# A 16-image hybrid network on one core: the first attention's instructions in another order, and layer-norm statistics written without a copy

## The chip, the core and the metric

The kernel runs on one core of one Trainium2 chip. The time is the device time of one execution in microseconds (us). TensorE (PE) does the matrix products, VectorE (DVE), ScalarE (ACT) and GpSimd (POOL) the elementwise work, SyncE (SP) issues DMAs. Each engine works through its own list of instructions in order; only semaphores order the lists against one another.

## The reference, cut to what matters

Sixteen images of 16x16 tokens with 96 channels pass six blocks: windowed attention with MLP, a convolution mixer with MLP, full attention, a binary FFN, causal attention, and four experts. The change touches the first block, and the statistics of most of the others. The first block is, for each image:

```
h = layernorm(x) * w + b                      # over 96 channels
windows of 8x8 tokens: 4 per image, 64 tokens each
qkv = h @ qkv_w + qkv_b                       # 12 heads of 8 channels
attn = softmax(q @ k^T / sqrt(8) + bias)      # 64 x 64 per head, bias by relative position
x = x + (attn @ v) @ proj_w + proj_b
```

Every later block begins with a layer norm of the new x, so each block, on adding its result to x, also takes mean and variance of it.

## The kernel before

**Layout.** x stays in SBUF as X, 32 tiles of 128 tokens; an image is two tiles. MV holds mean and variance of each tile. `statistics` (line 181) takes them after a residual has been added: per tile a bn_stats of X into stats, then per tile a bn_aggr into the small tile aggr, then, after a wait, one copy of aggr into MV, which raises the semaphore mv. `image_stats` (line 397) does the same for the input images of the first block, on semaphores of its own. GpSimd's `normalise` (line 138) waits for mv.

**The first attention** (`window_attention`, line 412) runs in half images. A half image u (0 to 31) is two windows, 128 rows; image n = u // 2. All engines run an outer loop over slots u, written out in full; in slot u each works on several images at different depths. By name:
- GpSimd `norm(n)`: the layer norm of image n into Y, then the projection's bias added to X (five instructions). The subtraction (line 463) takes the row maxima off the scores of u.
- TensorE `tokens_t(n)`: two transposes of Y into bank 0. `queries_keys(n)`: two projections into bank 1. `values(n)`: eight matmuls into bank 1. `scores(u)`: 12 matmuls into banks 3 to 5. `probs_t(u, b)`: three transposes of the probabilities (b = 0, 1: bank 6 or 2). `attend(u)`: 24 matmuls into bank 7. `outputs_t(n)`: two transposes into bank 0. `project(n)`: into bank 0.
- ScalarE: `tokens`, `queries`, `values`, `pt_out`, `out_t` copy these results out of the banks, and `exps(u)` is the exponential.
- VectorE: `keys_by_head(n)` spreads the keys over four masked copies. `biased_scores(u)` adds the position bias and then takes the maxima (lines 662 and 665). `heads_out(u)` divides by the sums. `residual(n)` adds the projection to X.

**Waits that matter here.** `tokens_t(n)` writes bank 0, which the projection of image n-4 still fills until its residual is read:

```
pe.wait_ge(s["y"], n + 1)
after(pe, s["hT"], n)
after(pe, s["x"], n - 4)
```

`scores(u)` waits until the add of u-1 has read banks 3 to 5, and the add of u waits for scores u. `values(n)` waits for queries n, which wait for the keys of n. `outputs_t(n)` waits for both heads of n. `project(n)` waits for out_t of n.

**Per image on VectorE before**, slot 2n and then 2n+1: image_stats n+4, residual n-3, add and maxima 2n, statistics n-3, heads 2n-3; add and maxima 2n+1, heads 2n-2, keys n+2.

**Per image on TensorE before**: scores 2n, both probs_t of 2n-2, attend 2n-3, tokens_t n+2, values n+1; scores 2n+1, probs_t of 2n-1 (first half), outputs_t n-2, probs_t (second half), queries_keys n+2, attend 2n-2, project n-2.

**Other users of statistics**: the two MLP stages (four tiles a step, in a hardware loop), the conv mixer (line 990, between two of the nine taps of the convolution on VectorE, ahead of `norm2`, whose chain runs over GpSimd's reciprocal root, `norm2b`, TensorE's `back` and ScalarE to the output matmuls and so to the next residual), the full attention (line 1304), the binary FFN (line 1478) and the causal attention (lines 1892 and 1905).

Of the kernel before, what the change touches and what calls it, by code (L numbers as in the profile page):

```python
# [22 lines left out]
ALU = mybir.AluOpType  # L23
# [114 lines left out]
def tiles_of(t, first, count):  # L138

    return t[:, bass.ds(first, count), :]  # L140
# [39 lines left out]

def statistics(dve, k, s, n, count):

    alone(dve, k)
    dve.wait_ge(s["x"], n + 1)
    after(dve, s["mv"], n)
    for t in range(count):
        last = dve.bn_stats(k.stats[:, t, :], k.X[:, bass.ds(n * count + t, 1), :])
    last.then_inc(s["bn"], 1)
    alone(dve, k)
    dve.wait_ge(s["bn"], n + 1)  # L190
    for t in range(count):
        last = dve.bn_aggr(k.aggr[:, t, :], k.stats[:, t, :])
    last.then_inc(s["ag"], 1)
    dve.wait_ge(s["ag"], n + 1)
    dve.tensor_copy(tiles_of(k.MV, n * count, count), k.aggr[:, 0:count, :]).then_inc(s["mv"], 1)
# [201 lines left out]
def image_stats(dve, k, s, i):  # L397

    dve.wait_ge(s[f"x{i // 4}"], 16 * 2 * WS)
    for t in range(2):  # L400
        last = dve.bn_stats(k.stats[:, t, :], k.X[:, 2 * i + t, None, :])
    last.then_inc(s["bn"], 1)
    dve.wait_ge(s["bn"], i + 1)
    for t in range(2):
        last = dve.bn_aggr(k.aggr[:, t, :], k.stats[:, t, :])
    last.then_inc(s["ag"], 1)
    dve.wait_ge(s["ag"], i + 1)
    dve.tensor_copy(tiles_of(k.MV, 2 * i, 2), k.aggr[:, 0:2, :]).then_inc(s["mv"], 1)
    dve.wait_ge(s["mv"], i + 1)


def window_attention(k, bank, begin):
# [3 lines left out]
    with ExitStack() as ctx:  # L416
# [19 lines left out]
        with nc.Block() as block:  # L436
# [8 lines left out]
            def _(pool):  # L445
# [13 lines left out]
                norm(2)  # L459
                for u in range(HALVES):  # L460
                    pool.wait_ge(s["mx"], u + 1)
                    x = S[u % 4]
                    pool.tensor_tensor(x[:], x[:], mx[u % 4][:].broadcast_to([P, H0, WTOK]), ALU.subtract).then_inc(s["sub"], 1)  # L463
                    if u % 2 == 0 and u // 2 + 3 < IMAGES:
                        norm(u // 2 + 3)
                pool.wait_ge(s["late"], 16 * len(k.late))
# [3 lines left out]
            def _(pe):  # L470
# [80 lines left out]
                for u in range(FIRST, LAST + 1):  # L551
# [3 lines left out]
                    if 0 <= u - 2 < HALVES:  # L555
                        probs_t(u - 2, 0)
                    if odd and 0 <= n - 2 < IMAGES:
                        outputs_t(n - 2)
                    if 0 <= u - 2 < HALVES:
                        probs_t(u - 2, 1)  # L560
                    if odd and n + 2 < IMAGES:
# [11 lines left out]
            def _(act):  # L573
# [38 lines left out]
                for u in range(FIRST, LAST + 1):  # L612
                    n, odd = u // 2, u % 2 == 1
                    if 0 <= u - 1 < HALVES:
                        exps(u - 1)
                    if not odd and 0 <= n + 1 < IMAGES:
                        queries(n + 1)
                    if 0 <= u - 2 < HALVES:
                        pt_out(u - 2, 0)
                    if odd and 0 <= n - 2 < IMAGES:  # L620
                        out_t(n - 2)
                    if 0 <= u - 2 < HALVES:
                        pt_out(u - 2, 1)
                    if not odd and n + 2 < IMAGES:
                        tokens(n + 2)
                    if not odd and 0 <= n + 1 < IMAGES:
                        values(n + 1)

            @block.vector
            def _(dve):  # L630
# [17 lines left out]
                def keys_by_head(n):  # L648
# [5 lines left out]
                                             op0=ALU.add, op1=ALU.mult).then_inc(s["kx"], 1)  # L654

                def biased_scores(u):
                    x = S[u % 4]
                    dve.wait_ge(s["sc"], u + 1)
                    if u == 0:
# [3 lines left out]
                                      k.bias0[:].rearrange("p (g j) k -> p g (j k)", g=3), ALU.add).then_inc(s["add"], 1)  # L663
                    dve.wait_ge(s["add"], u + 1)
                    dve.tensor_reduce(mx[u % 4][:, :, 0], x[:], AX.X, ALU.max).then_inc(s["mx"], 1)  # L665

# [12 lines left out]
                next(run)  # L679
                for u in range(FIRST, LAST + 2):  # L680
                    n, odd = u // 2, u % 2 == 1
                    if not odd and 3 <= n + 4 < IMAGES:
                        image_stats(dve, k, k.sem["set"], n + 4)
                    if not odd and 0 <= n - 3 < IMAGES:
                        residual(n - 3)
                    if 0 <= u < HALVES:
                        biased_scores(u)
                    if not odd and 0 <= n - 3 < IMAGES:
                        statistics(dve, k, s, n - 3, 2)
                    if 0 <= u - 3 < HALVES:  # L690
                        heads_out(u - 3)
                    if odd and n + 2 < IMAGES:
                        keys_by_head(n + 2)


def mlp(k, bank, prefix, w):
# [4 lines left out]
    with ExitStack() as ctx:  # L701
        G = [k.sb(f"{prefix}_G{i}", [P, KH, 512], F32, ctx) for i in range(2)]
        with nc.Block() as block:
# [44 lines left out]
            def _(dve):  # L748
                def residual(n):
                    dve.wait_ge(s["down"], n + 1)  # L750
                    dve.wait_ge(s["xb"], n + 1)
                    add_and_stats(dve, k, s, n, 4, bank[7][:, 0:4 * C].rearrange("p (t c) -> p t c", t=4))

# [1470 lines left out]
```

## Time and profile before

| what | value |
|---|---|
| time, median of 3 runs | 1306.49 us (1303.2 to 1314.98) |
| the profiled execution | 1309.46 us |
| its span, first to last instruction | 1307.7 us |
| mean granted TensorE clock | 0.942 of 2.4 GHz |
| TensorE busy | 1154.8 us (88%) |
| VectorE busy | 740.0 us (57%) |
| ScalarE busy | 515.9 us (39%) |
| GpSimd busy | 387.1 us (30%) |

The profiled execution is one run, 1.76 us longer than its span. The first attention lies from about 17 to 188 us in it, the first MLP to 247, the conv mixer to 407, the second MLP to 465, the full attention to 826, the binary FFN to 918, the causal attention and the experts to the end. A busy share over the span mixes stages with different limits. In the timeline a row is a start, a length, an engine and a line of the kernel; in brackets how long the engine sat idle before it, and which instruction's end ended that.

### The profile page before, as it was taken

What the parts mean: (1) busy time and instruction counts of PE and PEld (TensorE: products, weight loads), DVE (VectorE), ACT (ScalarE), POOL (GpSimd) and SP (SyncE); (2) the same over time, 40 slices, a digit from 0 to 9 for tenths busy, and PEclk for the clock granted to TensorE, in tenths of its full rate; (3) what the DMA queues carried; (4) which work ended last, traced back from release to release, by engine and by line L of the source; (5) the groups of instructions that cost most, each with busy time, mean ns of one, the idle gap of its engine ahead of it and who ended that gap; (6) DMA issues with size and microseconds to landing.
All of it is one profiled execution on the core that took longest, in us unless ns stands there. A gap on an engine that the chain in (4) does not pass through costs nothing. (4 is left out here: it accounts for less than half of the span.)

```text
span 1307.7 us, 23695 instructions
## 1 busy us (share of the span) xinstructions
PE 1154.8 (88%) x8859; PEld 790.6 (60%) x8859; DVE 740.0 (57%) x2112; ACT 515.9 (39%) x839; POOL 387.1 (30%) x584
## 2 busy tenths in 40 slices
PE   4888879789887979999999997788888978999998
PEld 2565656566665656766666674466455544577776
DVE  3788844477772436666666666276455565333322
ACT  1555533343431333333343332345343422455543
POOL 3645445443425421010101210424100000353522
PEclk8999969899997989999999998699799999999999
DMA  4500000000000000000000000000000000000000
GB/s 88 100 11 2 2 2 0 1 1 1 2 1 1 0 1 1 1 1 1 1 1 1 1 2 1 1 1 1 1 2 1 2 2 1 2 13 7 9 11 13
DMA packets 28924, 9.39 MB, mean 7 GB/s; under 512 B 26961, under 2 KB 28816, under 8 KB 28816
## 3 DMA queue, kind: packets, MB, share of 16 engines
q1 hardware_dynamic: 25760, 7.02, 2.6%
q8 instruction: 69, 1.13, 0.3%
q10 hardware_dynamic: 3056, 0.92, 0.3%
q14 instruction: 39, 0.32, 0.1%
HBM read 6.36 MB, written 1.57 MB: 6 GB/s over the span
## 5 line engine op out<-in xcount | busy, mean ns | idle before, releaser
L156 POOL TENSOR_TENSOR ln_v<-MV,eps 128x2 f32<-128x2 f32 (+3 forms) x81 | 16.2, 201 | 427.2 <-PE bank L1132 247.3
L1194 ACT ACTIVATE fa_e<-bank 128x1024 f32<-128x1024 f32 x64 | 65.5, 1024 | 161.1 <-PE bank L1102 161.1
L1997 PEld LDWEIGHTS bank<-e_w,ex_G 128*128 128x128 f32 x768 | 90.6, 192 | 14.4 <-issue 14.1
L2112 DVE SCALAR_TENSOR_TENSOR X<-bank,ex_L,X 128x96 f32<-128x96 f32 x128 | 31.8, 311 | 114.0 <-PE bank L1997 108.1
L1246 DVE TENSOR_REDUCE fa_z<-bank 128x4 f32<-128x1024 f32 x64 | 78.3, 1223 | 26.3 <-PE bank L1084 24.7
L1989 PE MATMUL bank<-hT,e_w 96*128 96x512 f32 x192 | 90.6, 609 | 0.0
L1997 PE MATMUL bank<-e_w,ex_G 128*128 128x96 f32 x768 | 90.0, 274 | 0.0
L2040 ACT ACTIVATE ex_G<-bank,e_b 128x512 f32<-128x512 f32 x96 | 64.3, 686 | 61.7 <-PE bank L1989 58.9
L1844 DVE TENSOR_REDUCE ca_z<-bank 128x2 f32<-128x256 f32 x96 | 48.9, 552 | 49.3 <-PE bank L1571 49.2
L1102 PE MATMUL bank<-fa_a,fa_b 64*128 64x256 f32 x512 | 74.1, 409 | 1.1 <-DVE fa_a L1253 1.1
L1115 PE MATMUL bank<-fa_e,fa_v 128*64 128x256 f32 x512 | 72.0, 404 | 1.1 <-ACT fa_e L1194 1.1
L159 POOL TENSOR_TENSOR ln_r<-ln_v,minus_half 128x2 f32<-128x2 f32 (+3 forms) x81 | 71.7, 885 | 0.0
L1762 ACT ACTIVATE ca_e<-bank 128x768 f32<-128x768 f32 x48 | 38.9, 810 | 78.9 <-PE bank L1571 78.9
L463 POOL TENSOR_TENSOR wa_s<-wa_s,wa_mx 128x768 f32<-128x768 f32 x32 | 47.1, 1471 | 73.8 <-DVE wa_mx L665 73.8
L1010 DVE SCALAR_TENSOR_TENSOR cm_acc<-cm_g,k_conv,cm_acc 128x256 f32<-128x256 f32 x128 | 66.1, 516 | 3.0
L1084 PE MATMUL bank<-fa_b,fa_a 64*128 64x256 f32 x512 | 66.0, 376 | 0.1
L1102 PEld LDWEIGHTS bank<-fa_a,fa_b 64*128 64x128 f32 x512 | 45.0, 190 | 29.4 <-issue 24.6
L1943 POOL TENSOR_TENSOR ex_tmp<-e_b,ex_L 128x384 f32<-128x384 f32 x8 | 6.7, 833 | 185.7 <-DVE ex_L L2100 185.7
L1557 PE MATMUL bank<-ca_b,ca_a 16*128 16x256 f32 (+1 forms) x384 | 47.4, 366 | 16.1 <-DVE ca_a L1853 15.7
L163 POOL TENSOR_TENSOR Y<-Y,ln_r 128x192 f32<-128x192 f32 (+3 forms) x81 | 56.1, 693 | 10.9
L1253 DVE TENSOR_TENSOR fa_a<-fa_a,bank 128x256 f32<-128x256 f32 x64 | 26.9, 421 | 56.3 <-PE bank L1092 56.3
L178 DVE TENSOR_TENSOR X<-X,bank 128x192 f32<-128x192 f32 (+2 forms) x56 | 23.6, 427 | 61.8 <-PE bank L719 43.0
(252 smaller groups left out, 2641.7 us busy)
## 6 DMA issues: line engine op xcount, KB each, us to landing
out_tokens<-X SPq DMA_DIRECT2D x8, 192.0 KB, 2.1
X<-in_x SPq DMA_DIRECT2D x56, 24.0 KB
e_w<-in_L_ffn_w SPq DMA_DIRECT2D x2, 576.0 KB
bias0r<-in_L_conv_rpb_table ACTq DMA_DIRECT2D x16, 24.0 KB
m0w<-in_L_conv_mlp_w SPq DMA_DIRECT2D x2, 144.0 KB
m1w<-in_L_conv_w SPq DMA_DIRECT2D x2, 144.0 KB
f_w<-in_L_ffn_W SPq DMA_DIRECT2D x2, 142.5 KB
mixer<-in_mixer SPq DMA_DIRECT2D x1, 256.0 KB
```

The source lines that it names most:

```text
L159: pool.tensor_tensor(r, v, k.minus_half[:, 0:count, :], ALU.pow).then_inc(s["rstd"], 1)
L163: pool.tensor_tensor(y, y, r.broadcast_to([P, count, C]), ALU.mult).then_inc(s["y"], 1)
L1010: dve.scalar_tensor_tensor(out=o, in0=src, scalar=kk, in1=o, op0=ALU.mult, op1=ALU.add).then_inc(s["conv"], 1)
L1084: last = pe.matmul(bank[b + i][:, c * TOK:(c + 1) * TOK], A[n % 2][rows, p, c * P:(c + 1) * P], B[n % 2][rows, p, :], start=True, stop=True)
L1102: last = pe.matmul(bank[b + i][:, c * TOK:(c + 1) * TOK], B[n % 2][rows, p, c * P:(c + 1) * P], A[n % 2][rows, p, :], start=True, stop=True)
L1115: last = pe.matmul(bank[4 + v % 2][64 * i:64 * i + 64, 0:TOK], V[n % 2][:, c, 2 * p + i, :], E[v % 2][:, i, c, :], start=(c == 0), stop=(c ...
L1194: act.activation(E[v % 2][:], k.banks[:, b:b + 2, :].rearrange("p i (c q) -> p i c q", c=2), ACT.Exp).then_inc(s["exp"], 1)
L1246: dve.tensor_reduce(Z[v % 2][:].rearrange("p c (i d) -> p i c d", i=2)[:, :, :, D2], k.banks[:, b:b + 2, :].rearrange("p i (c q) -> p i c ...
L1844: last = dve.tensor_reduce(dst, k.banks[:, 2 * p:2 * p + 2, c * P:(2 * c + 1) * P], AX.X, ALU.max, negate=True)
L1989: pe.matmul(bank[v % NB][:], k.ew1[:, e, j * P:(j + 1) * P], k.hT[slot][:], start=True, stop=True).then_inc(s["up"], 1)
L1997: last = pe.matmul(bank[4 + e % 2][:, t * C:(t + 1) * C], G[e % 2][:, j, t * P:(t + 1) * P], k.ew2[:, e, j, :], start=(j == 0), stop=(j == ...
L2040: act.activation(G[e % 2][:, j, :], bank[(KH * e + j) % NB][:], ACT.Gelu, bias=k.eb1[:, e, j:j + 1]).then_inc(s["gelu"], 1)
```

## The change

In the first attention, the lists are rearranged:
- VectorE, slot 2n: heads 2n-4, add 2n, keys n+1, maxima 2n, residual n-3; slot 2n+1: heads 2n-3, add and maxima 2n+1, statistics n-3, image_stats n+4. `maxima` becomes a function of its own.
- TensorE: outputs_t follows both halves of probs_t.
- ScalarE, slot 2n: pt_out (first half), exps 2n-1, pt_out (second half), queries n+1, tokens n+2; slot 2n+1: values n+1, pt_out, exps 2n, pt_out, out_t n-2.
- GpSimd: norm is written ahead of the subtraction of odd slots instead of behind that of even ones.

In `statistics` and `image_stats` bn_aggr writes straight into MV and raises mv; aggr, its wait and the copy fall away, except where `unrolled=False` is passed, which the MLP stages do. `image_stats` uses tiles 6 and 7 of stats.

```diff
@@ -178,7 +178,7 @@
     (dve.tensor_copy(x, new) if replace else dve.tensor_tensor(x, x, new, ALU.add)).then_inc(s["x"], 1)
 
 
-def statistics(dve, k, s, n, count):
+def statistics(dve, k, s, n, count, unrolled=True):
 
     alone(dve, k)
     dve.wait_ge(s["x"], n + 1)
@@ -188,6 +188,11 @@
     last.then_inc(s["bn"], 1)
     alone(dve, k)
     dve.wait_ge(s["bn"], n + 1)
+    if unrolled:
+        for t in range(count):
+            last = dve.bn_aggr(k.MV[:, n * count + t, :], k.stats[:, t, :])
+        last.then_inc(s["mv"], 1)
+        return
     for t in range(count):
         last = dve.bn_aggr(k.aggr[:, t, :], k.stats[:, t, :])
     last.then_inc(s["ag"], 1)
@@ -397,16 +402,14 @@
 def image_stats(dve, k, s, i):
 
     dve.wait_ge(s[f"x{i // 4}"], 16 * 2 * WS)
+    after(dve, s["mv"], i)
     for t in range(2):
-        last = dve.bn_stats(k.stats[:, t, :], k.X[:, 2 * i + t, None, :])
+        last = dve.bn_stats(k.stats[:, 6 + t, :], k.X[:, 2 * i + t, None, :])
     last.then_inc(s["bn"], 1)
     dve.wait_ge(s["bn"], i + 1)
     for t in range(2):
-        last = dve.bn_aggr(k.aggr[:, t, :], k.stats[:, t, :])
-    last.then_inc(s["ag"], 1)
-    dve.wait_ge(s["ag"], i + 1)
-    dve.tensor_copy(tiles_of(k.MV, 2 * i, 2), k.aggr[:, 0:2, :]).then_inc(s["mv"], 1)
-    dve.wait_ge(s["mv"], i + 1)
+        last = dve.bn_aggr(k.MV[:, 2 * i + t, :], k.stats[:, 6 + t, :])
+    last.then_inc(s["mv"], 1)
 
 
 def window_attention(k, bank, begin):
@@ -458,11 +461,11 @@
                 next(run)
                 norm(2)
                 for u in range(HALVES):
+                    if u % 2 == 1 and u // 2 + 3 < IMAGES:
+                        norm(u // 2 + 3)
                     pool.wait_ge(s["mx"], u + 1)
                     x = S[u % 4]
                     pool.tensor_tensor(x[:], x[:], mx[u % 4][:].broadcast_to([P, H0, WTOK]), ALU.subtract).then_inc(s["sub"], 1)
-                    if u % 2 == 0 and u // 2 + 3 < IMAGES:
-                        norm(u // 2 + 3)
                 pool.wait_ge(s["late"], 16 * len(k.late))
                 next_first_step(pool, k, s, IMAGES)
 
@@ -554,10 +557,10 @@
                         scores(u)
                     if 0 <= u - 2 < HALVES:
                         probs_t(u - 2, 0)
+                    if 0 <= u - 2 < HALVES:
+                        probs_t(u - 2, 1)
                     if odd and 0 <= n - 2 < IMAGES:
                         outputs_t(n - 2)
-                    if 0 <= u - 2 < HALVES:
-                        probs_t(u - 2, 1)
                     if odd and n + 2 < IMAGES:
                         queries_keys(n + 2)
                     if 0 <= u - 3 < HALVES:
@@ -611,20 +614,20 @@
                 act.wait_ge(s["pad"], 1)
                 for u in range(FIRST, LAST + 1):
                     n, odd = u // 2, u % 2 == 1
+                    if odd and 0 <= n + 1 < IMAGES:
+                        values(n + 1)
+                    if 0 <= u - 2 < HALVES:
+                        pt_out(u - 2, 0)
                     if 0 <= u - 1 < HALVES:
                         exps(u - 1)
+                    if 0 <= u - 2 < HALVES:
+                        pt_out(u - 2, 1)
+                    if odd and 0 <= n - 2 < IMAGES:
+                        out_t(n - 2)
                     if not odd and 0 <= n + 1 < IMAGES:
                         queries(n + 1)
-                    if 0 <= u - 2 < HALVES:
-                        pt_out(u - 2, 0)
-                    if odd and 0 <= n - 2 < IMAGES:
-                        out_t(n - 2)
-                    if 0 <= u - 2 < HALVES:
-                        pt_out(u - 2, 1)
                     if not odd and n + 2 < IMAGES:
                         tokens(n + 2)
-                    if not odd and 0 <= n + 1 < IMAGES:
-                        values(n + 1)
 
             @block.vector
             def _(dve):
@@ -653,6 +656,10 @@
                                              scalar=k.bk0[:], in1=k.headmask[:, :, None].broadcast_to([C, G4, TOK]),
                                              op0=ALU.add, op1=ALU.mult).then_inc(s["kx"], 1)
 
+                def maxima(u):
+                    dve.wait_ge(s["add"], u + 1)
+                    dve.tensor_reduce(mx[u % 4][:, :, 0], S[u % 4][:], AX.X, ALU.max).then_inc(s["mx"], 1)
+
                 def biased_scores(u):
                     x = S[u % 4]
                     dve.wait_ge(s["sc"], u + 1)
@@ -661,8 +668,6 @@
                     after(dve, s["pt"], 2 * u - 6)
                     dve.tensor_tensor(x[:].rearrange("p (g j) k -> p g (j k)", g=3), k.banks[:, 3:6, 0:G4 * WTOK],
                                       k.bias0[:].rearrange("p (g j) k -> p g (j k)", g=3), ALU.add).then_inc(s["add"], 1)
-                    dve.wait_ge(s["add"], u + 1)
-                    dve.tensor_reduce(mx[u % 4][:, :, 0], x[:], AX.X, ALU.max).then_inc(s["mx"], 1)
 
                 run = begin.vector(dve)
                 next(run)
@@ -677,20 +682,22 @@
                     last = dve.memset(t[C:P], 0.0)
                 last.then_inc(s["pad"], 1)
                 next(run)
-                for u in range(FIRST, LAST + 2):
+                for u in range(FIRST, LAST + 1):
                     n, odd = u // 2, u % 2 == 1
-                    if not odd and 3 <= n + 4 < IMAGES:
-                        image_stats(dve, k, k.sem["set"], n + 4)
+                    if 0 <= u - 4 < HALVES:
+                        heads_out(u - 4)
+                    if 0 <= u < HALVES:
+                        biased_scores(u)
+                    if not odd and 0 <= n + 1 < IMAGES:
+                        keys_by_head(n + 1)
+                    if 0 <= u < HALVES:
+                        maxima(u)
                     if not odd and 0 <= n - 3 < IMAGES:
                         residual(n - 3)
-                    if 0 <= u < HALVES:
-                        biased_scores(u)
-                    if not odd and 0 <= n - 3 < IMAGES:
+                    if odd and 0 <= n - 3 < IMAGES:
                         statistics(dve, k, s, n - 3, 2)
-                    if 0 <= u - 3 < HALVES:
-                        heads_out(u - 3)
-                    if odd and n + 2 < IMAGES:
-                        keys_by_head(n + 2)
+                    if odd and 3 <= n + 4 < IMAGES:
+                        image_stats(dve, k, k.sem["set"], n + 4)
 
 
 def mlp(k, bank, prefix, w):
@@ -749,7 +756,8 @@
                 def residual(n):
                     dve.wait_ge(s["down"], n + 1)
                     dve.wait_ge(s["xb"], n + 1)
-                    add_and_stats(dve, k, s, n, 4, bank[7][:, 0:4 * C].rearrange("p (t c) -> p t c", t=4))
+                    add_new(dve, k, s, n, 4, bank[7][:, 0:4 * C].rearrange("p (t c) -> p t c", t=4))
+                    statistics(dve, k, s, n, 4, unrolled=False)
 
                 def body(n, slot, first):
                     dve.wait_ge(s["T"], n + 1)
```

## Rows read from the trace of the kernel before

**Rows 1.** The stretches of the first attention; busy us of each engine, granted clock.
```profile
97.00:137.00 40.00, 32.82 (x445) 24.36 (x441) 35.59 (x87) 23.51 (x48) 21.55 (x29) 1.00 0.01 1
```

**Rows 2.** Timeline, one image, TensorE: start us, length us, engine, line.
```profile
104.70 0.88 PE L515 MATMUL bank<-ident,wa_s 128*128 128x128 f32 x6
...
106.66 0.40 PE L477 MATMUL bank<-ident,Y 128*96 128x128 f32 x2 [0.27 <-DVE X L178]
...
107.85 0.67 PE L505 MATMUL bank<-wa_kx,wa_q 32*64 32x256 f32 x12
...
108.45 0.55 PE L515 MATMUL bank<-ident,wa_s 128*128 128x128 f32 x3
...
110.43 0.42 PE L538 MATMUL bank<-ident,wa_a 128*96 128x128 f32 x2 [1.43 <-DVE wa_a L639]
...
110.69 0.49 PE L515 MATMUL bank<-ident,wa_s 128*128 128x128 f32 x3
...
111.01 0.59 PE L484 MATMUL bank<-wa_h,w_qkv 128*96 128x256 f32 x2
...
113.39 0.67 PE L505 MATMUL bank<-wa_kx,wa_q 32*64 32x256 f32 x12
```

**Rows 3.** Timeline, TensorE's scores later in the stage.
```profile
131.99 0.67 PE L505 MATMUL bank<-wa_kx,wa_q 32*64 32x256 f32 x12
...
142.90 0.67 PE L505 MATMUL bank<-wa_kx,wa_q 32*64 32x256 f32 x12
...
151.26 0.67 PE L505 MATMUL bank<-wa_kx,wa_q 32*64 32x256 f32 x12
...
167.10 0.67 PE L505 MATMUL bank<-wa_kx,wa_q 32*64 32x256 f32 x12
```

**Rows 4.** Timeline, the same image, VectorE.
```profile
104.04 1.27 DVE L652 SCALAR_TENSOR_TENSOR wa_kx<-bank,w_bk,headmask 96x1024 f32<-96x1024 f32 x1
...
106.16 0.35 DVE L178 TENSOR_TENSOR X<-X,bank 128x192 f32<-128x192 f32 x1
106.43 0.95 DVE L662 TENSOR_TENSOR wa_s<-bank,bias 128x768 f32<-128x768 f32 x1
...
107.41 0.95 DVE L665 TENSOR_REDUCE wa_mx<-wa_s 128x12 f32<-128x768 f32 x1
...
108.28 0.41 DVE L187 BATCH_NORM_STATS2 stats<-X 128x6 f32<-128x96 f32 x2
...
109.08 0.86 DVE L195 COPY MV<-aggr 128x4 f32<-128x4 f32 x1
```

**Rows 5.** Timeline, the same image, GpSimd's subtraction.
```profile
108.45 1.47 POOL L463 TENSOR_TENSOR wa_s<-wa_s,wa_mx 128x768 f32<-128x768 f32 x1 [3.94 <-DVE wa_mx L665]
```

**Rows 6.** Timeline, conv mixer, residual's statistics and the mixing matmuls.
```profile
305.30 1.57 PE L832 MATMUL bank<-cm_loc,mixer 128*128 128x192 f32 x8
...
306.66 0.17 DVE L195 COPY MV<-aggr 128x4 f32<-128x4 f32 x1
306.74 0.48 DVE L1010 SCALAR_TENSOR_TENSOR cm_acc<-cm_g,k_conv,cm_acc 128x256 f32<-128x256 f32 x1
...
307.14 0.62 DVE L972 BATCH_NORM_STATS2 cm_st<-bank 128x6 f32<-128x192 f32 x2
```

**Rows 7.** Timeline, VectorE near the attention's end.
```profile
167.86 0.96 DVE L662 TENSOR_TENSOR wa_s<-bank,bias 128x768 f32<-128x768 f32 x1 [0.30 <-PE bank L505]
```

**Rows 8.** Timeline, the same image, ScalarE.
```profile
109.95 0.84 ACT L582 ACTIVATE wa_s<-wa_s 128x768 f32<-128x768 f32 x1 [1.32 <-POOL wa_s L463]
...
110.82 0.49 ACT L578 ACTIVATE wa_pt<-bank 128x384 f32<-128x384 f32 x1
...
111.21 0.37 ACT L587 ACTIVATE wa_at<-bank 96x256 f32<-96x256 f32 x1
```

**Rows 9.** Timeline, start of the attention, values of image 2.
```profile
41.56 1.13 PE L490 MATMUL bank<-w_qkv,wa_h 128*128 128x96 f32 x8 [2.92 <-ACT wa_q L598]
```

**Rows 10.** Timeline, causal attention, VectorE's copy.
```profile
998.75 0.17 DVE L195 COPY MV<-aggr 128x8 f32<-128x8 f32 x1
```

## Prediction

> **What bounds the kernel now.** I read the page's busy times first (they stand in the table above): over the whole span TensorE is busy 88% and VectorE 57%. The change reorders one stage, so that share says little. The table of stretches shows the first attention in its steady part: VectorE 35.59 of 40 us, TensorE 32.82, at full granted clock [rows 1]. Here VectorE leads. TensorE's timeline shows one image as a cycle that repeats: from one start of the even slot's scores to the next but one 18.60 us (113.39 to 131.99), 9.30 us an image [rows 2, 3]. In that cycle TensorE idles twice: 0.27 us ahead of the token transposes, until VectorE's residual, and 1.43 us ahead of the transposes of the attention output, until VectorE's heads [rows 2]. A second proof lies in the stage itself. For the last images there is no image_stats left (two bn_stats, 0.41 us in the like pair of statistics [rows 4], two bn_aggr, a copy of 0.17 us as in [rows 6], two waits), and the cycle shrinks to 8.36 us (142.90 to 151.26) [rows 3]. Taking some 0.9 us off VectorE took 0.94 us off the cycle, so VectorE's own queue is the bound.
>
> **What is removed.** Every copy of aggr into MV in VectorE's statistics goes, except in the two MLP stages, which keep it. In the first attention the copy of statistics lasts 0.86 us and ends as GpSimd's subtraction ends (108.45 + 1.47 = 109.92; 109.08 + 0.86 = 109.94) [rows 4, 5]. In the conv mixer the same copy takes 0.17 us [rows 6]. So in the attention 0.7 us of it is being held by GpSimd. Its step is 0.78 us, since the next instruction may start 0.08 us before an end, and with it go 0.03 us of wait and 0.08 us of overlap; that of image_stats is about 0.2 us. VectorE's queue loses 1.0 to 1.1 us an image. If nothing else came to bind, the cycle would be 8.2 to 8.3 us.
>
> **What is moved, and what is not.** GpSimd's edit changes nothing. Before, the order is subtraction 2n, norm n+3, subtraction 2n+1; after, it is the same list, with norm written in the next slot ahead of its wait. "Heads first, one slot later" also gives the same neighbours for the odd heads. Three things do move on VectorE. Keys n+1 go from ahead of the add of slot 2n to between add and maxima. Residual n-3 goes from ahead of the add of 2n to behind its maxima. Statistics n-3 and image_stats go to the end of the odd slot, so the odd heads no longer stand behind them: the 1.43 us wait of TensorE goes.
>
> **What becomes late instead.** TensorE's tokens_t(n+2) waits for residual n-3, since both use bank 0, and behind it in TensorE's queue stand values n+1 and the scores of 2n+1. The add of 2n waits for the scores of 2n. So there is a loop: scores 2n, add, keys, maxima, residual, tokens_t, values, scores 2n+1, and all of TensorE's odd slot up to scores 2n+2. I add it up from starts, since an instruction that waits for nothing starts 0.08 us before its predecessor ends (maxima 0.95 us long at 107.41, the next at 108.28 [rows 4]):
> - scores 2n 0.67 [rows 2], plus 0.09 from their end to the add (167.10 + 0.67 = 167.77; 167.86) [rows 3, 7]: 0.76
> - add to keys 0.87, keys to maxima 1.27 - 0.08 = 1.19, maxima to residual 0.87, residual 0.35 [rows 4]: 3.28, so 4.04
> - residual to tokens_t 0.15 (106.16 + 0.35 = 106.51; 106.66) [rows 2, 4]: 4.19
> - tokens_t to scores 2n+1, 106.66 to 107.85: 1.19, so 5.38
> - scores to transposes, 107.85 to 108.45: 0.60, so 5.98
> - six probability transposes in one go, which the trace has only in the even slots: between twice the 0.32 of three (110.69 to 111.01) and the 0.88 that the six last [rows 2]. I take the middle, 0.76: 6.74
> - from the output transposes to the next scores, 110.43 to 113.39: 2.96, less the three transposes of 0.32 that now lie ahead of them: 2.64, so **9.38 us**, between 9.26 and 9.50.
>
> VectorE's own list is then 7.4 us of steps with some 1.5 us of wait for scores 2n+1 behind the residual (5.38 + 0.67 + 0.09 = 6.14, against 4.04 and heads of 0.43). It is no longer the bound, and the microsecond taken from it is spent as idle time. TensorE has one wait an image in place of two: from about 2.3 us (scores, six transposes, attend) to 4.19, some 1.9 us, against 0.3 + 1.4 to 1.6 before. Its work in the cycle hasn't changed, so the cycle can't move far.
>
> ScalarE's new order must fit into that. Its out_t(n-2) now stands behind exp and both probability copies. The first copy can start when three of the transposes are done, 5.98 + 0.5 = 6.5 (the values' copies are over by then); copy 0.49, exp 0.84 (GpSimd's subtraction is ready at 5.4), copy 0.49, out_t 0.37 [rows 8], less 0.08 for each overlap: 8.5. The projection needs it at 9.38 - 0.61 = 8.77. Hidden with 0.2 us to spare; without that cover each further 0.1 us is 0.1 us of cycle. Queries n+1 wait for the keys, which end at 2.9, and are over at 3.5, ahead of values at 4.4: hidden.
>
> **Sum over the first attention.** Images 3 to 11 each go from 9.30 (the first of them from 9.1) to 9.38: +0.9. The last two full cycles were 8.36 because image_stats was gone; the loop above holds no image_stats, so they stay at 9.38: 2 x 1.02 = +2.0. Two cycles of 10.9 us before (131.99 to 142.90 is one [rows 3]), with TensorE at the lower of its clocks (2.4 to 1.2 GHz), cost 1.6 us more than the others; I keep both, at the same price. Start-up: values 2 wait 2.92 us for queries 2 [rows 9]. These now stand behind one more probability copy (0.4), and the first maxima behind keys 1 (+0.4), which delays the subtraction, norm and exp in front of it: +0.8, between 0 and 1.6. The stage's end loses the last copy and its wait: -0.2. Sum: **+3.5 us**, between +1.5 and +5.5.
>
> **Sum elsewhere.** In the conv mixer residual's statistics lie inside VectorE's taps, ahead of norm2, and norm2 opens the chain over GpSimd and TensorE back to the next residual. Copy and wait there are 0.19 us (306.66 to 306.74 is 0.08, and 0.11 for the wait ahead of it and the overlap, as above) [rows 6]. Norm2 also waits for the mixing matmuls, which end at 305.30 + 1.57 = 306.87; it starts at 307.14 and would start at 306.95, just behind them. So all of it counts: 14 x 0.19 = 2.7, between 0 and 2.7. At the ends of the conv mixer, the full attention and the binary FFN the statistics are the last or next to last link: 3 x 0.2 = 0.6, less where setup hides it. In the causal attention the copy (998.75) stands straight ahead of the shift that TensorE waits for [rows 10]: 6 x 0.19 = 1.1, between 0 and 1.3. In the full attention TensorE is busy nearly without a gap: nothing. Sum: **-4.4 us**, between -1 and -4.6.
>
> **Net:** +3.5 - 4.4 = -0.9 us. The profiled execution took 1309.46 us, 1307.7 of it span; the median of the runs is 1306.49. By the profiled one 1308.6 us, by the median **1305.6 us**. About 1% (13 us) is what a measurement of this kernel can tell from no change, and the three runs shown alone span 12 us.
>
> **Rivals.**
> - *VectorE stays the bound.* If the residual were not what tokens_t waits for last, the cycle would follow VectorE to 8.3 us. For: the 8.36 us cycles [rows 3]. Against: the wait is in the code, and it is already the 0.27 us in front of tokens_t now [rows 2]. It would give 8 x 1.0 + 2 x 0.9 = -10, and with -4.4 elsewhere 1292 us. Chance 0.11.
> - *Slower: TensorE's clock falls in every cycle.* The single wait of 1.9 us is followed by token transposes, and the odd slot now has eight transposes in a row. If that makes the clock fall once in each image, each costs the 1.6 us of the 10.9 us cycle [rows 3]. Nine cycles that are now at full clock give +14.4, net +13.5, or 1320 us. It decides from some five cycles on (+8 against the -0.9, outside my range of error). Against: the present cycle has waits of the same sum, and stretches of 30 us and more at clock 1.00 [rows 1]. Chance 0.06.
> - *The conv mixer doesn't follow*, since the mixing matmuls end 0.08 us before norm2 would start, or the causal copies are covered: only the attention's loss counts, +3.5 - 1 = +2.5, or 1309 us. Chance 0.2.
> - *My forecast*: 0.63.
>
> On the second rival the Trainium skill, TensorE: Matmul & The Clock Gate, section "Part 4: PE-mode transpose", says that transposes do not count as activity for the clock as other matmuls do. That speaks against putting the output transposes behind all six. By it the second rival would be the likely one, 1320 us; the present even slots, six transposes in one go at clock 1.00, do not show it so far.
>
> **How the numbers follow.** Forecast and third rival are both within 1%: 0.83. The first rival straddles the bound at 1293.4, so with other gains of that kind faster is 0.11; slower 0.06. The forecast's own bounds run from +1.5 - 4.6 = -3 to +5.5 - 1 = +4.5, that is 1303 to 1311, and the median of a few runs adds 3 us either way. Widened toward the two outer cases: 1296 to 1314.
>
> **What would show it.** After: a cycle of 9.3 to 9.5 us between scores of one parity, also for the images without image_stats; TensorE idle 1.6 to 2.0 us ahead of tokens_t for VectorE's residual, and none ahead of the output transposes; VectorE idle about 1.5 us behind the heads, for scores; conv mixer cycles 0.19 us shorter. Wrong if the wait ahead of tokens_t stays at 0.3 us, if cycles fall to 8.3, if the projection waits for out_t by more than 0.1 us, or if the granted clock drops inside most cycles.

## The result, and the profile after

| what | before | after |
|---|---|---|
| median | 1307.69 us (1303.2 to 1314.98, 4 runs) | 1328.58 us (1321.81 to 1332.5, 4 runs) |
| ratio after / before | | 1.0149, 95% interval 1.008 to 1.0218 |
| the profiled execution, its span | 1309.46, 1307.7 us | 1324.93, 1323.1 us |
| granted TensorE clock, mean | 0.942 | 0.925 |
| TensorE busy | 1154.8 us | 1171.9 us |
| VectorE busy | 740.0 us, 2112 instructions | 721.4 us, 2035 instructions |

The change makes the kernel slower by 1.5%. VectorE has 77 instructions and 18.6 us less, as meant; TensorE, which got no new work, is busy 17 us longer at a lower clock. Where the time lies is read from the starts of stages in the timeline (the second tap of the conv mixer, first row sums of the full and of the causal attention, the end). First attention with first MLP: +22.8 us. Conv mixer with second MLP: 225.0 to 221.6, -3.4. Full attention with binary FFN: 434.1 to 429.6, -4.5. The rest: 395.2 to 395.7, +0.5. Sum +15.4, the difference of the spans.

So the loss is in the first attention. TensorE's timeline of the kernel after, one image and a bit; it answers to [rows 2]:

```profile
102.83 0.52 PE L480 MATMUL bank<-ident,Y 128*96 128x128 f32 x2 [1.88 <-DVE X L178]
103.15 1.86 PE L493 MATMUL bank<-w_qkv,wa_h 128*128 128x96 f32 x8
104.94 1.14 PE L508 MATMUL bank<-wa_kx,wa_q 32*64 32x256 f32 x12
106.02 1.54 PE L518 MATMUL bank<-ident,wa_s 128*128 128x128 f32 x6
107.35 0.63 PE L541 MATMUL bank<-ident,wa_a 128*96 128x128 f32 x2
...
111.11 0.67 PE L508 MATMUL bank<-wa_kx,wa_q 32*64 32x256 f32 x12
...
115.28 0.40 PE L480 MATMUL bank<-ident,Y 128*96 128x128 f32 x2 [1.89 <-DVE X L178]
115.51 1.03 PE L493 MATMUL bank<-w_qkv,wa_h 128*128 128x96 f32 x8
116.47 1.07 PE L508 MATMUL bank<-wa_kx,wa_q 32*64 32x256 f32 x12
117.47 1.54 PE L518 MATMUL bank<-ident,wa_s 128*128 128x128 f32 x6
...
122.02 0.67 PE L508 MATMUL bank<-wa_kx,wa_q 32*64 32x256 f32 x12
```

The one wait of 1.9 us for VectorE's residual is there, and none stands ahead of the output transposes (L541): the queues do what was forecast. The cycle doesn't: from 111.11 to 122.02 it is 10.91 us. Look at the same instruction in two places. The scores take 0.67 us at 111.11 and 1.14 at 104.94, the six transposes 0.87 elsewhere and 1.54 here. The table of stretches says why (columns: stretch, its length, busy us of PE, PEld, DVE, ACT, POOL, granted clock, DMA share, GB/s):

```profile
65.00:145.00 80.00, 66.80 (x721) 50.37 (x715) 50.05 (x125) 37.59 (x77) 36.89 (x49) 0.79 0.02 5
101.00:104.00 3.00, 1.17 (x7) 1.20 (x7) 2.09 (x5) 1.53 (x4) 1.49 (x2) 0.83 0.01 3
104.00:110.00 6.00, 6.00 (x40) 4.06 (x40) 3.04 (x10) 2.70 (x7) 3.77 (x6) 0.52 0.00 0
110.00:113.00 3.00, 3.00 (x58) 2.32 (x56) 1.62 (x4) 0.71 (x2) 0.00 (x0) 1.00 0.00 0
```

After the wait TensorE is busy without a gap, at 0.52 of its clock (1.2 GHz, but for the edge) for six us, then it is back at 1.00 (2.4 GHz). The clock falls so behind each of the waits of 1.88 or 1.89 us, but it doesn't stay down equally long. Here is the fall behind the next wait, two us a row (columns: stretch, its length, busy us of PE, granted clock, DMA share, GB/s):

```profile
116.00:118.00 2.00, 2.00 (x20) 0.66 0.04 8
118.00:120.00 2.00, 2.00 (x9) 0.50 0.00 0
120.00:122.00 2.00, 2.00 (x31) 0.99 0.00 0
```

These rows come to 3.4 us at the lower level, the like rows of the fall at 103 us to 6.8. From the even scores of slot 6 to those of slot 28 the eleven cycles are 9.28, 12.45, 10.91, 10.84, 12.45, 10.91, 10.83, 12.45, 10.91, 10.83, 12.50 us, sum 124.36: six with the shorter fall, four with the longer one, and one without, behind a wait of 1.67 us. Before, there were nine between 8.35 and 9.30 and two of 10.9, sum 103.41.

VectorE's timeline of the same slots, which answers to [rows 4]:

```profile
100.30 1.27 DVE L655 SCALAR_TENSOR_TENSOR wa_kx<-bank,w_bk,headmask 96x1024 f32<-96x1024 f32 x1
101.49 0.94 DVE L661 TENSOR_REDUCE wa_mx<-wa_s 128x12 f32<-128x768 f32 x1
102.35 0.34 DVE L178 TENSOR_TENSOR X<-X,bank 128x192 f32<-128x192 f32 x1
...
106.17 0.96 DVE L669 TENSOR_TENSOR wa_s<-bank,bias 128x768 f32<-128x768 f32 x1 [3.05 <-PE bank L508]
...
108.03 0.41 DVE L187 BATCH_NORM_STATS2 stats<-X 128x6 f32<-128x96 f32 x2
108.55 0.25 DVE L193 BATCH_NORM_AGGREGATE MV<-stats 128x2 f32<-128x6 f32 x2
```

Keys and maxima now stand ahead of the residual, which ends at 102.69 and lets tokens_t go at 102.83. The copy is gone. VectorE then idles 3.05 us for scores that TensorE computes at half its clock.

### The profile page after: what moved, and what is told of

Read it like the earlier page. It is cut to its first block and busy times, and to the rows that moved or that the text cites. A ratio compares the mean times of both kernels' runs of the same rounds, so it can differ in the third digit from the quotient of the medians.

```text
span 1323.1 us, 23628 instructions
## 1 busy us (share of the span) xinstructions
PE 1171.9 (89%) x8859; PEld 806.4 (61%) x8859; DVE 721.4 (55%) x2035; ACT 514.2 (39%) x839; POOL 386.2 (29%) x584
## 2 busy tenths in 40 slices
DMA packets 28924, 9.38 MB, mean 7 GB/s; under 512 B 26962, under 2 KB 28817, under 8 KB 28817
## 3 DMA queue, kind: packets, MB, share of 16 engines
q8 instruction: 69, 1.13, 0.3%
## 5 line engine op out<-in xcount | busy, mean ns | idle before, releaser
L163 POOL TENSOR_TENSOR Y<-Y,ln_r 128x192 f32<-128x192 f32 (+3 forms) x81 | 56.1, 693 | 10.9
L669 DVE TENSOR_TENSOR wa_s<-bank,bias 128x768 f32<-128x768 f32 x32 | 30.6, 957 | 51.3 <-PE bank L508 51.3
```

## Experiments

Eleven kernels, each timed against the kernel before. "Cycle" is the time between the scores of two even slots in the steady part; "clock" is the granted clock of the stretch from 65 to 145 us (before 0.96, after 0.79).

| run | against | ratio to before, 95% | span us | cycle us | clock |
|---|---|---|---|---|---|
| e1 residual first | after | 0.9833 (0.9782 to 0.9884) | 1301.0 | 8.44 | 0.98 |
| e2 six products in the wait | after | 0.9969 (0.9935 to 1.0003) | 1303.5 | 9.28 | 1.00 |
| e3 copies out, old order | before | 0.9768 (0.9722 to 0.9815) | 1275.1 | 8.03 | 1.00 |
| e4 new order, copies in | after | 1.0181 (1.0123 to 1.0238) | 1328.5 | 10.8 to 12.6 | 0.80 |
| e5 eight transposes in the wait | after | 0.9943 (0.9917 to 0.9969) | 1308.0 | 9.28 | 1.00 |
| e6 three products in the wait | after | 0.9965 (0.9939 to 0.9992) | 1305.8 | 9.28 | 1.00 |
| e7 e1, keys in the old place | e1 | 0.9778 (0.9738 to 0.9818) | 1286.8 | 8.17 | 1.00 |
| e8 e3, two new lists | e3 | 0.9776 (0.9733 to 0.9818) | 1284.8 | 8.17 | 1.00 |
| e9 e7, ScalarE's old list | e7 | 0.9788 (0.9750 to 0.9826) | 1280.2 | 7.66, 7.82 | 1.00 |
| e10 e3, TensorE's new list | e3 | 0.9766 (0.9715 to 0.9817) | 1275.8 | 7.8 | 1.00 |
| e11 four products in a wait of before | before | 0.9968 (0.9939 to 0.9996) | 1298.0 | 9.30 | 1.00 |

My theory after the result: the loop through the residual is as forecast, and its single long wait makes the clock fall. The rivals: the loop itself is longer than added up; the direct bn_aggr into MV costs something; the rearranged lists of TensorE or ScalarE are late. Each expectation quoted says which of them it sets against which.

**e1, the residual back ahead of the add.** This takes the wait away, and all else of the change stays.

```diff
+                    if not odd and 0 <= n - 3 < IMAGES:
+                        residual(n - 3)
                     if 0 <= u < HALVES:
                         biased_scores(u)
...
                         maxima(u)
-                    if not odd and 0 <= n - 3 < IMAGES:
-                        residual(n - 3)
```

> The changed kernel with one line moved: residual(n-3) stands ahead of the add of slot 2n again, as in the kernel before; all else as changed. Theory A (the single wait of 1.88 us for the residual lets TensorE's clock fall in every image): the token transposes find the residual done; TensorE's longest wait becomes the one of values for queries and keys, about 1.0 us; clock 1.00 in most cycles; the cycle is the path scores 0.76, keys 0.87 + 1.27, queries 0.6, values to scores 0.96, the odd slot 4.0: 8.5 us. Some -12 us in the attention and -4 elsewhere against the kernel before: about 1292 us, clearly faster than before. Rival B (the new order of the other lists, ScalarE's out_t behind both copies or the output transposes behind all six, makes the slow cycles): the cycle stays at 10.9 to 12.4 us and the time near 1328 us.

TensorE's timeline of e1:

```profile
114.07 0.42 PE L480 MATMUL bank<-ident,Y 128*96 128x128 f32 x2
115.32 1.13 PE L493 MATMUL bank<-w_qkv,wa_h 128*128 128x96 f32 x8 [0.82 <-ACT wa_q L601]
116.38 0.67 PE L508 MATMUL bank<-wa_kx,wa_q 32*64 32x256 f32 x12
```

tokens_t no longer waits, the clock falls in one steady cycle (10.07 us) and not in the ten others of that part, and the kernel is 1.7% faster than before. The place of one instruction of 0.35 us is the whole loss. A new wait of 0.82 us shows: values wait for the queries, which wait for the moved keys. But e1 alters both the loop and the wait, so it doesn't tell whether the clock or the loop is at fault.

**e2, e5, e6: the wait filled.** Here the loop stays as in after, and idle work goes into the wait: products into bank 3 that nobody reads, begun when the add of 2n has read the bank and overwritten by the scores of 2n+1. The diff of e2; e6 has 3 for 6, e5 eight transposes of the identity.

```diff
                     if not odd and n + 2 < IMAGES:
+                        if n >= 3:
+                            pe.wait_ge(s["add"], u + 1)
+                            keep_warm(pe, k, bank[3][:], 6)
                         tokens_t(n + 2)
```

> The changed kernel with six idle products of 512 columns put into TensorE's wait for the residual, on bank 3 once the add has read it. Order and waits of all else are as changed. Theory A (clock): the work of 6 x 0.22 = 1.3 us fits into the wait of 1.88 us, so the path through the residual isn't longer, and the clock stays up: cycle 9.3 us as in the one cycle of the changed kernel that ran at full clock (55.79 to 65.07), the attention about 23 us shorter than in the changed kernel, time about 1305 us. Rival B (order of the other lists): more work on TensorE can't shorten anything, 1328 us or more.

> As the kernel with the filled wait, but the filling is eight transposes of the identity (about 1.2 us) in place of six bf16 products. Theory A1 (the clock falls because TensorE stands still for 1.9 us in one piece): any instructions hold the clock, the cycle is 9.3 us and the time about 1305 us. Theory A2 (as the Trainium skill has it in TensorE: Matmul & The Clock Gate, Part 4: PE-mode transpose, transposes do not count as activity): the clock falls as in the changed kernel, cycles of 11 us, about 1328 us.

> As the kernel with the filled wait, but three products (0.65 us) in place of six, so that about 1.2 us of the wait stay empty. The kernel before had an empty wait of 1.43 us in each cycle and a clock of 1.00 in 7 of 9. Theory A: the clock holds here in most cycles too, cycle 9.3 us, 1305 to 1310 us. If the clock needed the whole wait filled, the time would be near 1328 us.

e2, TensorE's timeline, and then its row in the table of stretches:

```profile
119.71 0.67 PE L508 MATMUL bank<-wa_kx,wa_q 32*64 32x256 f32 x12
...
121.93 1.47 PE L129 MATMUL bank<-causal,identb 128*128 128x512 bf16 x6
123.89 0.39 PE L480 MATMUL bank<-ident,Y 128*96 128x128 f32 x2 [0.48 <-DVE X L178]
124.12 1.03 PE L493 MATMUL bank<-w_qkv,wa_h 128*128 128x96 f32 x8
125.08 0.67 PE L508 MATMUL bank<-wa_kx,wa_q 32*64 32x256 f32 x12
...
128.99 0.67 PE L508 MATMUL bank<-wa_kx,wa_q 32*64 32x256 f32 x12
```

```profile
65.00:145.00 80.00, 75.66 (x944) 53.38 (x943) 60.68 (x151) 46.69 (x96) 45.01 (x60) 1.00 0.02 6
```

and e5 and e6, the filler and the wait left behind it:

```profile
115.06 1.09 PE L572 MATMUL bank<-ident 128*128 128x128 f32 x8
117.02 0.40 PE L480 MATMUL bank<-ident,Y 128*96 128x128 f32 x2 [0.86 <-DVE X L178]
```

```profile
116.16 0.82 PE L129 MATMUL bank<-causal,identb 128*128 128x512 bf16 x3
118.11 0.40 PE L480 MATMUL bank<-ident,Y 128*96 128x128 f32 x2 [1.13 <-DVE X L178]
```

In all three every steady cycle is 9.28 us (119.71 to 128.99), the one unfilled full-clock cycle of after. More work for TensorE, and the kernel is 1.8 to 2.0% faster than after (0.9969, 0.9943 and 0.9965 of before, against 1.0149). So the loop isn't at fault and the clock is: 1.88 us of idle in one piece ahead of tokens_t, once an image, and the clock falls behind it, for 1.6 or 3.2 us of cycle; with 1.13 us or less it stays at 1.00. Transposes fill as well as products.

**e11, the same in the kernel before.** Its two cycles of 10.9 us I had taken as given. Four products of 1.03 us stand ahead of outputs_t, where it idles 1.43 us [rows 2].

```diff
                     if odd and 0 <= n - 2 < IMAGES:
+                        if n + 2 < IMAGES:
+                            pe.wait_ge(s["v"], n + 2)
+                            keep_warm(pe, k, bank[1][:], 4)
                         outputs_t(n - 2)
```

> The kernel before, with four idle products (0.9 us) put into TensorE's wait of 1.43 us for the heads, on bank 1 once the values are out of it. Nothing else changes. Theory: the two cycles of 10.9 us in the kernel before are the same fall of the clock; they become 9.3 us, and the attention shortens by 3 us; all cycles stay 9.30 us, since VectorE sets them. Rival: the falls of the clock come from elsewhere and stay.

```profile
114.32 1.03 PE L129 MATMUL bank<-causal,identb 128*128 128x512 bf16 x4
115.91 0.42 PE L538 MATMUL bank<-ident,wa_a 128*96 128x128 f32 x2 [0.56 <-DVE wa_a L642]
```

No 10.9 us cycle is left, the steady ones stay at 9.30, and the median moves by 0.3%, about what two cycles of 1.6 us would give (3.2 of 1307). In the kernel before both falls stand right behind a wait of 1.43 us: TensorE idles until 90.23 and until 138.33, and the clock is below 1.00 in just these two stretches of the steady part (columns as in the first table of stretches):

```profile
90.00:97.00 7.00, 6.77 (x79) 5.09 (x79) 4.55 (x12) 3.56 (x8) 3.47 (x5) 0.76 0.01 4
137.00:143.00 6.00, 4.67 (x43) 3.55 (x49) 3.51 (x8) 2.94 (x5) 4.57 (x7) 0.72 0.02 4
```

Six other waits of 1.43 us passed without a fall. So the kernel before stood near the same edge; with two falls in one trace and none in one of e11, this is less firm than what e2, e5 and e6 show.

**e3 and e4, the two halves of the change apart.** e3 is the kernel before with only the copies taken out (the first two hunks of the diff of the change); e4 is the kernel after with the copies put back (`unrolled=False` throughout, the old `image_stats`).

> The kernel before in its old order, with the copies of the statistics taken out as in the change (the MLP stages keep theirs). The forecast said that VectorE bounds the old order: the cycle then goes from 9.30 to about 8.25 us, the conv mixer's from 8.98 to 8.76; -10 to -11 us in the attention and -4 elsewhere: about 1292 us. If the copy in the attention is covered by something else (TensorE's wait for the heads, for example, ends with another path), only the conv mixer and the causal attention gain: 1303 us.

> The changed kernel with the copies of the statistics put back everywhere: the reordering alone. Theory A: VectorE has idle time in the new order, so the copies there cost little, the wait for the residual is unchanged and the clock falls as in the changed kernel; the conv mixer and the rest lose their 4 us again: about 1332 us. If the missing copy is what makes the clock fall (VectorE is done earlier and TensorE's pattern of waits changes), it would be near 1310 us.

e4 still waits 1.89 us for the residual and has after's cycles: the direct bn_aggr has no part in the loss. e3 is the better half, 2.3% faster than before. Its VectorE and two of its even scores:

```profile
98.95 0.41 DVE L187 BATCH_NORM_STATS2 stats<-X 128x6 f32<-128x96 f32 x2
99.46 0.25 DVE L193 BATCH_NORM_AGGREGATE MV<-stats 128x2 f32<-128x6 f32 x2
99.62 0.20 DVE L640 RECIPROCAL wa_rec<-bank 128x12 f32<-128x12 f32 x1
```

```profile
95.11 0.67 PE L508 MATMUL bank<-wa_kx,wa_q 32*64 32x256 f32 x12
...
103.14 0.67 PE L508 MATMUL bank<-wa_kx,wa_q 32*64 32x256 f32 x12
```

The residual's statistics take 0.67 us to the next instruction; before 1.58, so 0.91 less. In image_stats it is 0.93 to 0.60, 0.33 less. Together 1.24, and the cycle went from 9.30 to 8.03, 1.27: VectorE is the bound in this order, us for us. I had expected a cycle of 8.25 and 1292 us; the median is 1279.8. The slots 6 to 28 give 16.0 of the 32.6 us of e3's span, 3.2 of it because the two falls of the clock are gone; the start gives 1.3, attention's end with the MLP 5.6 (there the clock is 0.69 and 0.79 in the two tens from 160 to 180 us, and was 0.62, 0.50 and 0.68 in the three from 170 to 200 before), conv mixer 2.7, full attention 7.1. In the last I had expected no gain from the copies, and it isn't theirs: with the copies in the stage takes 434.1 us (before), 428.9 (e4) and 430.4 (e11, where nothing behind the first attention is altered), without them 427.0 (e3) to 435.6 (e7, e8). It goes with the granted clock of the stage, 0.95 where it takes 432 us or more, 0.97 in e3, e4 and e11. One profiled execution can't price the copies there, and some 7 us of e3's span are of this kind.

**e7 to e10: which of the other moves cost.** e7 puts the keys of e1 back to the end of the odd slot, and e9 gives e7 ScalarE's old list as well. From the other side, e8 is e3 with after's lists of ScalarE and TensorE, e10 e3 with TensorE's alone.

```diff
-                    if not odd and 0 <= n + 1 < IMAGES:
-                        keys_by_head(n + 1)
...
                         image_stats(dve, k, k.sem["set"], n + 4)
+                    if odd and n + 2 < IMAGES:
+                        keys_by_head(n + 2)
```

> The kernel with the residual first, and the keys too in their old place (keys n+2 at the end of the odd slot). Of the new VectorE order only statistics and image_stats at the end of the odd slot and the single list of heads stay. In the kernel with the residual first TensorE waits 0.82 us an image for queries behind keys, and VectorE 1.09 us for scores. Theory: both waits go, TensorE is the bound, the cycle is 7.6 to 7.9 us against 8.44 there and 8.03 in the kernel without copies: 1275 to 1280 us. Rival: the end of the odd slot gets so long on VectorE (statistics, image_stats, heads, keys) that the add of the next slot comes late: 8.2 us or more, 1285 us.

> The kernel without copies in the old order, with ScalarE's and TensorE's lists as changed (output transposes behind both halves, out_t behind both copies, values first in the odd slot); VectorE's list stays old. Theory A (only VectorE's moves did the harm): within 0.2 us of the 8.03 us cycle, 1278 to 1285 us. Rival B (the lists of ScalarE and TensorE have a share): the projection waits for out_t, cycle 8.5 us or more, 1290 us or more.

> The kernel with residual and keys in their old places, and ScalarE's list as in the kernel before (queries right behind the exponential, ahead of both probability copies). There the values of TensorE waited 0.26 us for queries in a cycle of 8.17 us, and reached TensorE 3.20 us after the scores, against 2.62 us in the kernel without copies. Theory: ScalarE's new list held queries back; the path scores to values shrinks to about 2.6 us, TensorE has no wait left, cycle 7.6 us, 1273 to 1279 us. Rival: something else than queries sets 8.17 us; the cycle stays there and the time at 1284 us.

> The kernel without copies in the old order, with TensorE's list alone as changed (output transposes behind both halves of the probability transposes). In its cycle of 8.03 us TensorE waited 0.22 us for the heads ahead of the output transposes. Theory: the three transposes fill that wait, the cycle is 7.7 to 7.9 us and the time 1276 to 1280 us, equal to the kernel without copies within what can be measured. Rival: ScalarE's out_t, in its old place ahead of the second probability copy, now waits for the later transposes and holds that copy and the attention product up: 8.1 us or more.

The values in e1 waited 0.82 us. In e7:

```profile
115.00 1.13 PE L493 MATMUL bank<-w_qkv,wa_h 128*128 128x96 f32 x8 [0.26 <-ACT wa_q L601]
```

In e8:

```profile
116.00 1.13 PE L493 MATMUL bank<-w_qkv,wa_h 128*128 128x96 f32 x8 [0.55 <-ACT wa_q L601]
```

And in e9, one cycle of TensorE:

```profile
117.05 0.67 PE L508 MATMUL bank<-wa_kx,wa_q 32*64 32x256 f32 x12
...
119.57 0.42 PE L480 MATMUL bank<-ident,Y 128*96 128x128 f32 x2
119.89 1.13 PE L493 MATMUL bank<-w_qkv,wa_h 128*128 128x96 f32 x8
...
124.87 0.67 PE L508 MATMUL bank<-wa_kx,wa_q 32*64 32x256 f32 x12
```

e7's cycle, 8.17 us, missed the 7.6 to 7.9 that I expected, and the rival's figure, 8.2, came by another way than the rival's: with the keys early the wait is shorter and not gone, since the queries stand behind both copies of the probabilities in ScalarE's new list. e9 with the old list has no wait there and cycles of 7.66 and 7.82 (117.05 to 124.87). Its median, 1281.7 us, is above the 1273 to 1279 expected; in its profiled execution the stages from the full attention on take 828.7 us, in e3 with the same instructions 822.3. e8 shows the same from the old side: 8.17, against 8.03 in e3 and 7.8 in e10. So TensorE's new list is worth 0.2 us a cycle, ScalarE's costs 0.35 to 0.5, and VectorE's order e7 has (heads first, residual ahead of the add) is no worse than the old one. In the medians the five kernels e3, e7, e8, e9 and e10 can't be told apart (0.9766 to 0.9788). Each is 2.1 to 2.3% faster than before and, by the ratios, some 3.7% faster than after; e3, the smallest edit, is the one to keep.

## Why the prediction was wrong

Predicted 1305.6 us (1296 to 1314), measured 1328.6. Step by step:

- **VectorE bounds the old order: right.** e3 takes 1.24 us off its queue and 1.27 off the cycle.
- **The copies, 1.0 to 1.1 us an image: somewhat small.** It is 1.24. The residual's part is 0.91, forecast at 0.8 to 0.9, and the small copy of image_stats 0.33, not 0.2.
- **GpSimd's edit changes nothing: right.** Its instructions run in the same order.
- **The loop, 9.38 us (9.26 to 9.50): right at full clock.** 9.28 in after's one such cycle and in all steady ones of e2, e5 and e6. Its parts too: tokens_t waits 1.88 (forecast 1.6 to 2.0), the output transposes not at all, and VectorE idles 1.66 us for the odd scores in e2 (some 1.5).
- **The failed step: "Its work in the cycle hasn't changed, so the cycle can't move far."** I set one wait of 1.9 us against two of 0.3 and 1.4 to 1.6, by their sum. TensorE's work is the same in instructions and not in time: behind the single wait it runs at 0.50 for 3.4 or 6.8 us. Ten of eleven cycles average 11.51 us, 2.23 above the loop, +22.3; the loop itself gives -1.3 against before's 103.41, which holds two such cycles. Together +20.95, where I had +2.9. The cycle from slot 28 to 30, which the sum left out, went from 7.49 to 9.38.
- **The rival that came: TensorE's clock falls in every cycle.** Mechanism and place were named. Both numbers were off: 0.06 was too little for what the rows showed, and the price was 1.6 us on nine cycles. 1.6 holds in six of the ten; in the four with the longer fall it is 3.2, on average 2.23, so 1320 and not 1329. I held "waits of the same sum, and stretches of 30 us and more at clock 1.00" against it. That evidence was about another wait: no wait of 1.9 us stood in it, and the two cycles of 10.9 us, which I carried over "at the same price", were the warning: the clock falls right behind the 1.43 us wait in both, and e11, with that wait shortened, has none.
- **The rule on transposes.** By the Trainium skill, TensorE: Matmul & The Clock Gate, section "Part 4: PE-mode transpose", that transposes don't count as activity as other matmuls do, I called the second rival the likely one, though its chance stayed 0.06. The rival came, but not by that rule, as far as e5 bears: eight fp32 transposes in the wait kept the clock at 1.00, as three or six products did, with the six probability transposes still in one go in all of them.
- **Queries hidden, ScalarE's list hidden with 0.2 us to spare: right only behind the residual's wait.** out_t held nothing. Once the long wait is gone, the keys' move and the queries' cost 0.82 us (e1), the queries alone 0.26 and 0.55 (e7, e8).
- **Start-up +0.8: too much.** From the first scores to those of slot 6 it is 25.46 against 25.33, +0.1.
- **Conv mixer, 14 x 0.19: right, a little small.** VectorE's timeline of after, answering to [rows 6]:

```profile
318.87 0.36 DVE L178 COPY X<-bank 128x192 f32<-128x192 f32 x1 [0.47 <-PE bank L861]
319.31 0.42 DVE L187 BATCH_NORM_STATS2 stats<-X 128x6 f32<-128x96 f32 x2
319.84 0.25 DVE L193 BATCH_NORM_AGGREGATE MV<-stats 128x2 f32<-128x6 f32 x2
...
320.37 0.62 DVE L980 BATCH_NORM_STATS2 cm_st<-bank 128x6 f32<-128x192 f32 x2
...
327.63 0.36 DVE L178 COPY X<-bank 128x192 f32<-128x192 f32 x1 [0.47 <-PE bank L861]
```

  8.76 us a cycle (318.87 to 327.63) where it was 8.98, so -0.22. The stage with its MLP fell by 3.4, in e4 with the copies by 0.8: 2.6 belong to the copies. That is all that the runs show of the -4.4 elsewhere; that these stages together fell by 7.4 is not the forecast come true.
- **Causal attention -1.1: not seen.** Causal attention and experts took 395.7 us after 395.2. It was one row and a sum over it. With the same instructions this part takes 394.3 us in e10 and 398.4 in e9, so the traces can't show a gain of 1.1, and whether there is one stays open.
- **Full attention, nothing: not contradicted.** -4.5 measured, and -5.2 with the copies in (e4). The stage differs by up to 8.6 us between kernels that run the same instructions in it, with the granted clock, so this isn't the removal's.

## What to carry to other kernels

Don't compare the idle time of TensorE by its sum: list each wait with its length in one piece, and treat a change that joins two into a longer one as a change of the clock, priced by the kernel's own slow cycles and multiplied by all cycles. Ahead of moving an instruction in one queue, ask who waits for the buffer that it frees; here 0.35 us of VectorE's work put behind 2.9 us of other work (add, keys, maxima) cost 3.1% of the kernel (0.9833 of before in e1, 1.0149 in after). When two edits come as one, time them apart: one half here was worth -2.3%, the other +1.8%, and the two together +1.5% and not -0.5%, since the time that the first takes off VectorE turns into waiting in the order of the second.

## What the runs showed of the hardware

- One idle piece of 1.88 us in each 9.3 us cycle, with TensorE otherwise busy, brought the granted clock to 0.50 in each of ten cycles, at a cost of 1.6 us in six of them (3.4 us at 0.50) and 3.2 in four (6.8 us); the eleventh, with a wait of 1.67 us, kept 1.00. With 1.13, 0.86 or 0.48 us left it was 1.00 throughout the steady part; with eight waits of 1.43 us, and one of 0.27 between them, it fell behind two (before); with one of 0.82 in one of eleven cycles (e1). What decides between these isn't settled by the runs.
- Filling idle time with products that nobody reads made the kernel faster: 1.47 us of them an image gave 1.8% against after (e2), with the loop as long as it was at full clock.
- Eight fp32 transposes (1.09 us) in the wait held the clock at 1.00, as six or three bf16 products did (e5; e2, e6).
- The same instructions of the full attention and the binary FFN took 427.0 us at a mean granted clock of 0.97 (e3) and 435.6 at 0.95 (e7, e8).
- A copy of 4 columns on VectorE took 0.86 us beside GpSimd's subtraction and 0.17 elsewhere; with its waits its removal gave back 0.91.
